# Layer 3's causal mask added to the scores on TensorE, and constant rows written in another block

## The reference

```python
q, k, v = x @ Wq.T + bq, x @ Wk.T + bk, x @ Wv.T + bv        # 16 heads of 8
scores = einsum('bhqd,bhkd->bhqk', q, k) / sqrt(8)
bias = -slopes[:, None, None] * abs(pos[:, None] - pos[None, :])
scores = scores + where(pos[:, None] >= pos[None, :], bias, -inf)
out = einsum('bhqk,bhkd->bhqd', softmax(scores), v)
return out.reshape(b, l, 128) @ Wo.T + bo
```

## Time and profile before

| | us |
|---|---|
| median of three runs | 2795.85 (2792.22 to 2800.66) |
| the profiled execution | 2813.61 |
| its span | 2811.9 |
| PE busy | 2098.0 (75%) |
| DVE busy | 1478.0 (53%) |
| ACT busy | 1163.6 (41%) |
| POOL busy | 395.0 (14%) |

### The profile page before, as it was taken

How to read it: one execution, slowest core, us unless ns; L and a number is a source line. 1 busy time by engine, 2 the same in 40 slices (tenths; PEclk the granted TensorE clock), 3 DMA queues, 4 the chain that set the end, 5 groups by cost and what they waited for, 6 DMA issues and landing times. The chain is left out here.

```text
span 2811.9 us, 41151 instructions
## 1 busy us (share of the span) xinstructions
PE 2098.0 (75%) x14039; PEld 1347.6 (48%) x14039; DVE 1478.0 (53%) x3920; ACT 1163.6 (41%) x2345; POOL 395.0 (14%) x474
## 2 busy tenths in 40 slices
PE   3313897546913889999999999996773068989976
PEld 2202796434912445555555555553662034444445
DVE  4628222252244656767777676773443455666524
ACT  0112453123410556666666666663221013555542
POOL 1260003513040341000000000000003520000000
PEclk9855898757955999999999999998997555897878
DMA  4310562114512100000000000001452131322001
GB/s 125 122 48 0 194 232 76 36 53 158 196 32 106 37 31 9 1 1 1 1 1 1 1 1 1 1 1 53 165 187 76 36 105 57 99 67 86 27 10 30
DMA packets 133972, 173.15 MB, mean 62 GB/s; under 512 B 16728, under 2 KB 93632, under 8 KB 133328
## 3 DMA queue, kind: packets, MB, share of 16 engines
q1 hardware_dynamic: 123104, 144.52, 15.9%
q0 software_dynamic: 10240, 20.99, 2.5%
q10 hardware_dynamic: 432, 5.11, 0.4%
HBM read 68.06 MB, written 45.15 MB: 40 GB/s over the span
## 5 line engine op out<-in xcount | busy, mean ns | idle before, releaser
L1845 ACT ACTIVATE t_p<-t_p,t_low 128x512 f32<-128x512 f32 x512 | 369.5, 722 | 327.1 <-DVE t_low L1916 321.1
L1916 DVE CUSTOM_DVE_ANT_0 t_p<-bank,L2t_skewed 128x512 f32<-128x512 f32 x512 | 332.6, 687 | 289.1 <-PE bank L1738 266.2
L127 PE MATMUL pair<-ident,t_p 128*128 128x128 f32 x2048 | 282.2, 280 | 18.7 <-ACT t_p L1845 6.6
L127 PEld LDWEIGHTS pair<-ident,t_p 128*128 128x128 f32 x2048 | 219.5, 141 | 115.6 <-issue 106.1
L2245 ACT ACTIVATE alibi_p<-pair 128x1024 f32<-128x1024 f32 (+1 forms) x192 | 168.8, 883 | 185.2 <-PE pair L2132 184.9
L2304 DVE CUSTOM_DVE_ANT_0 alibi_junk<-bank,alibi_later 128x512 bf16<-128x512 f32 (+1 forms) x256 | 150.8, 622 | 105.5 <-PE bank L2144 103.0
L1996 POOL COPY t_wide<-t_inverse 128x512 f32<-128x512 f32 x64 | 39.2, 613 | 893.5 <-DVE t_inverse L1932 884.6
L2144 PE MATMUL bank<-alibi_k_aug,alibi_q_aug 32*128 32x512 f32 (+1 forms) x256 | 107.7, 584 | 35.3 <-DMA alibi_k_aug<-aug_k 15.8
L1738 PE MATMUL bank<-t_k_hi,t_q_hi 64*128 64x512 f32 x512 | 129.7, 503 | 3.7 <-DVE t_low L1916 3.4
L1738 PEld LDWEIGHTS bank<-t_k_hi,t_q_hi 64*128 64x128 f32 x512 | 48.3, 185 | 162.2 <-issue 150.5
L1760 PE MATMUL pair<-t_pT,t_v 128*64 128x512 f32 x512 | 123.8, 605 | 1.5 <-DVE t_hT L1939 1.5
(11 more groups left out here) (478 smaller groups left out, 4458.4 us busy)
## 6 DMA issues: line engine op xcount, KB each, us to landing
L0moe_w<-L_packed SPq DMA_DIRECT2D x39, 578.0 KB, 3.2
L2moe_w<-L_packed SPq DMA_DIRECT2D x39, 450.0 KB, 2.9
L1moe_w<-L_packed SPq DMA_DIRECT2D x23, 578.0 KB, 3.3
alibi_q_aug<-aug_q SPq DMA_DIRECT2D x8, 1024.0 KB, 7.4
alibi_k_aug<-aug_k SPq DMA_DIRECT2D x8, 1024.0 KB, 7.6
L2t_skewed<-bias_table SPq DMA_DIRECT2D x16, 448.0 KB, 8.7
slots<-g ACTq DMA_DIRECT2D x3, 1664.0 KB, 10.2
L0moe_xs<-slots SPq DMA_DIRECT2D x39, 128.0 KB, 3.0
```

The source lines that it names most:

```text
L127: last = nc.tensor.transpose(out[0:piece.shape[1], j * P:j * P + piece.shape[0]], piece, ident[0:piece.shape[0], 0:piece.shape[0]])
L1845: nc.scalar.activation(p[:, u % RING, :], p[:, u % RING, :], ACT.Exp, bias=low[:, u % 16:u % 16 + 1], scale=-1.0, accum_out=sums[:, n % 2, ...
L1916: nc.vector.tensor_tensor_reduce(out=p[:, u % RING, :], in0=score_ps[h][:], in1=skewed[:, (n % PAIRS) * 2 + h, start:start + SEQ], scale=- ...
```

## The change

The constant rows are made and stored in `spread_bias_block` instead of `setup_block`, in tiles of their own: POOL's part behind the flip matrix, DVE's behind the spreading and before the turning, SP's four stores and the wait for them behind the wait for the skewed loads.

In layer 3 the maxima are plain reductions, one for a `tops_second`. The causal mask is added to every score job by PE: `hides` issues four parts of 128, 96, 64 and 32 columns (for each block of the job) in the job's own row strip, interleaved with the parts of the veils, and the last part adds one to `scored`. The full-array `hide` matmul, the tiles `later` and `junk`, and DVE's fills for them are gone. POOL makes `one`, `veil` and the new `shade` before its first `low_part`.

```diff
@@ setup_block @@
-        steady = [k.s[0:HEADS].rearrange("p t d -> p (t d)").rearrange("p (r n) -> p r n", r=8),
-                  k.xnT[0:HEADS].rearrange("p (r n) -> p r n", r=8)]
...
-            sp.wait_ge(rows_filled, 9)
-            for side in range(2):
-                for e in range(2):
-                    sp.dma_start(k.aug_dram[side][e, :, 24:32, :], steady[side]).then_inc(steady_stored, 16)
-            sp.wait_ge(steady_stored, 64)
...
-            for h in range(HEADS):
-                nc.gpsimd.memset(slope[:, 0, h:h + 1], high[h]).then_inc(slopes_set, 1)
-                nc.gpsimd.memset(slope[:, 1, h:h + 1], rest[h]).then_inc(slopes_set, 1)
-            pool.wait_ge(slopes_set, 2 * HEADS)
-            nc.gpsimd.affine_select(out=slope[:], in_=slope[:], compare_op=ALU.is_equal, fill=0.0, base=0,
-                                    pattern=[[0, 2], [-1, HEADS]], channel_multiplier=1).then_inc(slope_made, 1)
...
-            dve.wait_ge(slope_made, 1)
-            nc.vector.tensor_reduce(column[:, 0:2], slope[:], AX.X, ALU.add).then_inc(slope_summed, 1)
...
@@ spread_bias_block @@
+        steady = [st.sb(f"steady{j}", [HEADS, 8, SEQ])[:] for j in range(2)]
...
             sp.wait_ge(read, 16 * HEADS)
+            sp.wait_ge(rows_filled, 9)
+            for side in range(2):
+                for e in range(2):
+                    sp.dma_start(k.aug_dram[side][e, :, 24:32, :], steady[side]).then_inc(steady_stored, 16)
+            sp.wait_ge(steady_stored, 64)
...
+            dve.wait_ge(slope_made, 1)
+            nc.vector.tensor_reduce(column[:, 0:2], slope[:], AX.X, ALU.add).then_inc(slope_summed, 1)
+            dve.wait_ge(slope_summed, 1)
+            nc.vector.tensor_scalar(column[:, 2:4], column[:, 0:2], -1.0, None, ALU.mult).then_inc(slope_summed, 1)
+            dve.wait_ge(slope_summed, 2)
+            for j in range(2):
+                for row, col in ((1 - j, 2 * j), (3 - j, 2 * j + 1)):
+                    nc.vector.tensor_copy(steady[j][:, row, :], column[:, col:col + 1].to_broadcast([HEADS, SEQ])).then_inc(rows_filled, 1)
...
@@ alibi_attention_block, PE @@
+                w = 32 * (part + 1)
+                for c, a, e in regions(quad):
+                    for r in (2 * half, 2 * half + 1):
+                        ins = nc.tensor.matmul(flip_ps[u % 2][:, r % 2, a:a + w], one[rows(r), part, :], veil[rows(r), part, 0:w],
+                                               start=False, stop=True, skip_group_check=True)
+                if part == 3:
+                    ins.then_inc(flipped, 1)
...
                 bank = score_bank(s)
                 w = (t + 1) * P
                 nc.tensor.matmul(bank[:, 0:w], q_aug[rows(r), b % AUG, G, t * P:w], k_aug[rows(r), b % AUG, G, 0:w],
-                                 start=True, stop=True).then_inc(scored, 1)
+                                 start=True, stop=True, skip_group_check=True)
...
             def scores_first(b, s, r):
                 bank = score_bank(s)
-                if b == 0:
-                    pe.wait_ge(hide_laid, 1)
-                nc.tensor.matmul(bank[:].rearrange("p (g n) -> p g n", n=P), hide[:],
-                                 k.before[:].unsqueeze(1).to_broadcast([P, GROUPS, P]), start=True, stop=True)
                 for g in range(GROUPS):
-                    ins = nc.tensor.matmul(bank[:, g * P:(g + 1) * P], q_aug[rows(r), b % AUG, g, 0:P],
-                                           k_aug[rows(r), b % AUG, g, 0:P], start=False, stop=True,
-                                           skip_group_check=True)
-                ins.then_inc(scored, 1)
+                    nc.tensor.matmul(bank[:, g * P:(g + 1) * P], q_aug[rows(r), b % AUG, g, 0:P],
+                                     k_aug[rows(r), b % AUG, g, 0:P], start=(g == 0), stop=True, skip_group_check=True)
+
+            def hide(s, r, part, blocks, period, first):
+
+                out = score_ps[s % 2][:].rearrange("p (g n) -> p g n", n=period)[:, 0:blocks, first + 32 * part:first + P]
+                mask = shade[rows(r), part, 32 * part:P].unsqueeze(1).to_broadcast([32, blocks, P - 32 * part])
+                ins = nc.tensor.matmul(out, one[rows(r), part, :], mask, start=False, stop=True, skip_group_check=True)
+                if part == 3:
+                    ins.then_inc(scored, 1)
...
+            def hides(b, m, part):
+                s, G, kind, other = score_index(b, m), m // 6, m % 6, 2 * (1 - m % 2)
+                if b == 0 and m == 0 and part == 0:
+                    pe.wait_ge(veiled, 12)
+                if kind < 4:
+                    t = 3 - kind // 2
+                    hide(s, other, part, 1, SEQ, t * P)
+                    hide(s + 1, other + 1, part, 1, SEQ, t * P)
+                else:
+                    hide(s, other + G % 2, part, 2, 2 * P, P)
+                    if first_row(m) is not None:
+                        hide(s + 1, first_row(m), part, GROUPS, P, 0)
...
                     b, m = score_tick(n, j)
                     if 0 <= b < NB:
                         scores(b, m)
-                    if 0 <= n < NB:
-                        veils(n, j)
+                    for part in range(4):
+                        if 0 <= n < NB:
+                            veils(n, j, part)
+                        if 0 <= b < NB:
+                            hides(b, m, part)
@@ alibi_attention_block, VectorE @@
             def tops_one(b, s, G, r, t):
-                w, h = (t + 1) * P, 4 * G + r
+                h = 4 * G + r
                 dve.wait_ge(scored, s + 1)
-                nc.vector.tensor_tensor_reduce(out=junk[:, s % 2, 0:w], in0=score_ps[s % 2][:, 0:w], in1=later[:, SEQ - w:SEQ], scale=1.0,
-                                               scalar=-HUGE, op0=ALU.add, op1=ALU.max, accum_out=top[:, t, h:h + 1]).then_inc(maxed, 1)
+                nc.vector.tensor_reduce(top[:, t, h:h + 1], score_ps[s % 2][:, 0:(t + 1) * P], AX.X, ALU.max).then_inc(maxed, 1)
 
             def tops_second(b, s, G, r):
                 dve.wait_ge(scored, s + 1)
-                for g in range(2):
-                    h, half = 4 * (G + g) + r, slice(g * 2 * P, (g + 1) * 2 * P)
-                    ins = nc.vector.tensor_tensor_reduce(out=junk[:, s % 2, half], in0=score_ps[s % 2][:, half],
-                                                         in1=later[:, SEQ - 2 * P:SEQ], scale=1.0, scalar=-HUGE, op0=ALU.add,
-                                                         op1=ALU.max, accum_out=top[:, 1, h:h + 1])
-                ins.then_inc(maxed, 1)
+                nc.vector.tensor_reduce(top[:, 1, :].rearrange("p (g r) -> p g r", r=4)[:, G:G + 2, r],
+                                        score_ps[s % 2][:].rearrange("p (g n) -> p g n", n=2 * P), AX.X, ALU.max).then_inc(maxed, 1)
...
-            nc.vector.tensor_scalar(hide[:], k.ident[:], LOWEST, None, ALU.mult).then_inc(hide_laid, 1)
-            nc.vector.memset(later[:, 0:SEQ - P], 0.0).then_inc(later_laid, 1)
-            nc.vector.tensor_scalar(later[:, SEQ - P:SEQ], k.before[:], LOWEST, None, ALU.mult).then_inc(later_laid, 1)
-            dve.wait_ge(later_laid, 2)
@@ alibi_attention_block, GpSimd @@
+            nc.gpsimd.memset(one[:], 0.0).then_inc(cleared, 1)
+            nc.gpsimd.memset(veil[:], 0.0).then_inc(cleared, 1)
+            nc.gpsimd.memset(shade[:], 0.0).then_inc(cleared, 1)
+            pool.wait_ge(cleared, 3)
+            for r in range(4):
+                nc.gpsimd.affine_select(out=one[rows(r)], in_=one[rows(r)], compare_op=ALU.not_equal, fill=1.0, base=0,
+                                        pattern=[[-32, 4], [1, P]], channel_multiplier=-1).then_inc(veiled, 1)
+                nc.gpsimd.affine_select(out=veil[rows(r)], in_=veil[rows(r)], compare_op=ALU.is_ge, fill=LOWEST, base=0,
+                                        pattern=[[-32, 4], [1, P]], channel_multiplier=-1).then_inc(veiled, 1)
+                nc.gpsimd.affine_select(out=shade[rows(r)], in_=shade[rows(r)], compare_op=ALU.is_ge, fill=LOWEST, base=0,
+                                        pattern=[[32, 4], [-1, P]], channel_multiplier=1).then_inc(veiled, 1)
+            pool.wait_ge(veiled, 12)
             low_part(0, 0, q_cut, q_low)
             low_part(0, 1, k_cut, k_low)
             nc.gpsimd.memset(v_aug[:], 0.0).then_inc(ones_cleared, 1)
             pool.wait_ge(ones_cleared, 1)
             nc.gpsimd.memset(v_aug[:].rearrange("p e t h c -> p (e t h) c")[:, :, W:W + 1], 1.0).then_inc(ones_laid, 1)
-            nc.gpsimd.memset(one[:], 0.0).then_inc(cleared, 1)
...
```

More of the change, by code:

```diff
@@ L2071, in alibi_attention_block @@
         full, hi, lo = (st.sb(n, [P, 2, SEQ]) for n in ("full", "hi", "lo"))
-        later, junk = st.sb("later", [P, SEQ]), st.sb("junk", [P, 2, SEQ], BF16)
-        hide = st.sb("hide", [P, P], BF16)
-        one, veil = st.sb("one", [P, 4, P], BF16), st.sb("veil", [P, 4, P], BF16)
```

(46 more changed lines are left out.)

42 lines of the change are left out of this document (17 added, 25 removed).

## The result

The changed kernel took 2856.14 us (median of 4 runs, 2842.91 to 2862.26) beside 2795.86 of the kernel before: a ratio of 1.0207 (95% interval 1.0175 to 1.024), **+60 us** (+49 to +67) where +49 was forecast. Its profiled execution took 2851.98 us with a span of 2850.2, +38.4 against the span of before. So the two profiled executions stand nearer to each other than the medians: that of the kernel before took 18 us more than its median, that of the changed kernel 4 us less than its own.

A forecast was written before the change was run, and what follows sets the result against it. Setup was held by the constant-row stores, the attention's first 32 ticks by a PE-VectorE ping-pong, its 1.2 GHz middle by PE. Terms -17 + 7 + 22 + 21 + 7 + 9 = +49 on 2795.85 gave 2845 us; range 2813 to about 2905.

The forecast's parts named there:

- Constant rows out of setup, -17: Setup block: without the four stores it ends near 18.1 us instead of 35.0, -17 us, bounds -17 and -13.
- Into the bias block, 0: Bias block: making and storing the constant rows there costs 0, with 9 us of cover; +7 if stores took twice as long.
- Start of the attention, +7: Layer 3's attention start: GpSimd makes three masks before its first `low_part`, so the first scores come 7 us later.
- The loop of a tick: Layer 3's attention: a joint post makes each tick one closed loop; six ticks 13.9 us at 1.2 GHz, 11.0 at 2.4.
- First 32 ticks, +22: Attention ticks before the first exponentials, all at 1.2 GHz: 76 us against 54.4, +22 us.
- Ticks at 2.4 GHz, +0.20 each: Middle of layer 3's attention: 106 ticks at 2.4 GHz each 0.20 us longer, +21 us; bounds 0.08 and 0.4 each.
- Ticks at 1.2 GHz, +0.13 each: Middle of layer 3's attention: 54 ticks at 1.2 GHz each 0.13 us longer, +7 us; bounds 0 and +22.
- Clock, +9: Layer 3's attention: longer ticks leave PE less dense, 14 more ticks fall to 1.2 GHz, +9 us; bounds 0 and +60.
- 2 (masks cost nothing): Rival on layer 3's attention: slack takes the masks up, leaving -17 + 7, 2786 us; 5%.
- 1 (faster by the clock): Rival on layer 3's attention: masks fill idle strips, PE is granted 2.4 GHz throughout, 2780 us; 7%.
- 4 (the clock falls for most of the middle): Rival on the attention's middle: 160 ticks at 2.57 us, +82 in place of +37, 2890 us; 12%.
- 3 (strips don't overlap): Rival on PE's masks: added matmuls start one behind the other, about +35 us, 2880 us; 15%.

The follow-up runs named there:

- experiment 5: The changed kernel run again (2859.47 us, ratio 1.0237), and with GpSimd's first two low parts ahead of the masks' making (2847.82 us, ratio 1.021).
- Experiment 2: Kernel before with constant rows moved and both score jobs posted by the second's last matmul; old maxima, no masks on PE: 2833.49 us, ratio 1.0187.
- experiment 7: The changed kernel with all veils of a tick issued ahead of all its masks, not interleaved: 2843.87 us, ratio 1.0181.
- low parts early: The changed kernel with GpSimd's first two low parts ahead of the masks' making; on chip C 2826.92 us, ratio 1.0182.
- chip B: Chip on which the unaltered changed kernel was run again: 2859.47 us, ratio 1.0237 to the kernel before.
- The order alone: The kernel of Experiment 2, rows moved and one joint post without masks on PE: 2833.49 us, ratio 1.0187; again on another chip 2828.58 us, ratio 1.0187.
- experiment 3: The changed kernel with each tick's second score and its masks after the first score's masks and the veils, a post per bank: 2854.32 us, ratio 1.0224.
- experiment 6: Kernel before with constant rows moved and the veils between a tick's two scores, no masks on PE: 2771.98 us, ratio 0.9897.
- experiment 8: On one chip, The order alone again (2828.58 us, ratio 1.0187) beside the changed kernel with low parts early (2826.92 us, ratio 1.0182).
- The doubled kernel: The changed kernel with every added mask matmul issued twice, order unchanged: 2919.03 us, ratio 1.0488.
- the rows alone: Kernel before with only the constant rows moved as in the change, maxima and masks as before: 2771.47 us, ratio 0.996.

## Why the prediction was right

**Constant rows out of setup, -17:** -16.5, by both traces. The last fetch stayed hidden.

**Into the bias block, 0:** as long as before to within 0.1 us.

**Start of the attention, +7:** +7.3, and experiment 5 shows the mechanism.

**The loop of a tick:** six ticks forecast at 13.9 us at 1.2 GHz, 14.07 measured; the first tick 2.45 (forecast 2.46), 384 columns 2.07 (2.07). **First 32 ticks, +22:** +23.0. Experiment 2 splits it: 14.2 the order, 8.8 the masks' work.

**Ticks at 2.4 GHz, +0.20 each:** +0.25 in the profiled execution (1.77 to 2.01), and 2.00 to 2.02 in three others; with 110 ticks +27 where +21 stood. With whole ticks alone it is +0.18 to +0.22, so the size is right within the counting. The loop itself came to 2.07 against 2.05. The exponential, whose post comes later behind the masks (experiment 7), may add to it; that is argued and not isolated.

**Ticks at 1.2 GHz, +0.13 each:** +0.15, but the level was wrong: I took 2.44 us from one stretch of before, and all its stretches give 2.73. So 49 ticks ran at this clock, not 54: +7, as forecast.

**Clock, +9:** the pair of profiled executions denies it (0.79 before and 0.81 after in the middle). Without it the terms come to +48 and the spans to +38; of the 10 us between, 5 lie in the last 32 ticks (47.3 to 42.2, at a clock of 1.00, where I had said "as before"), 2 ahead of the attention and 2 in the middle. The runs affirm the term: with the masks a kernel had 39 us (chip C, low parts early) to 69 (chip B) more at 1.2 GHz than before. The terms above account for 23 + 7 of it, and on chip B for the 7 of the start too, which lie at a clock of 0.50. So 9 to 32 us are left, 3 to 11 ticks at 0.86, **+3 to +10**. The size was right, with luck in it, as the middle without any change there differed by 18 us between two traces. My reason was not right: I reasoned that longer ticks leave PE less dense. The order alone moves some 35 ticks to 1.2 GHz. The masks' work behind the joint post brings most of them back, all but some 3 on chip C and some 10 on chip B; yet with a post for each bank the same work moves some 45 ticks the other way (experiments 3 and 6). Nor is it long waits: PE's longest idle time in the middle was 1.24 us before, 0.68 in the change and 0.33 in experiment 3, and the clock fell in all three. And PE's busy share in the middle doesn't sort the kernels: 92% both before (302.6 of 327.9 us) and in experiment 8's order alone (333.6 of 361.1), 95% with masks, and 99% (388.45 of 392.2) in experiment 3, whose clock was the lowest. What the clock follows stays open.

**The sum:** -16.5 + 7.3 + 23.0 + 27 + 7 + 3 to 10 = +51 to +58, beside a measured +60 (+49 to +67). So the step that carried the forecast, one post for both banks making a tick one closed loop, is shown in the first 32 ticks and in the pace at 2.4 GHz. It is not shown that without it the masks would have been cheap.

**The rivals.** 2 (masks cost nothing) is refuted. Behind a joint post their work adds nothing to the whole (experiment 8, within 10 us), but with a post for each bank it adds 3.3% (experiment 3 beside 6). The two costs don't add up: either alone brings about nearly the whole loss. 1 (faster by the clock) fails, as the middle's clock was 0.81 to 0.85; 4 (the clock falls for most of the middle) fails for the change. It comes nearest in experiment 3, where 74 of 159 ticks ran at 1.2 GHz. 3 (strips don't overlap) fails: where both strips of a tick stream at once, the masks of six ticks are 4 x 320 + 1280 + 640 = 3200 columns one behind the other, 2.66 us at 0.83 ns and 14.2 over 32 ticks; one strip after the other they would be 5120, and 22.7. The doubled kernel took 14.2 more. The Trainium skill's floor of about 25 ns from start to start ("TensorE: Matmul & The Clock Gate", section "Wait — 56ns, not 53.3ns?") would put a tick's 7.3 added matmuls at 0.18 us at either clock; the doubling added 0.26 at 2.4 GHz and 0.44 in the first 32 ticks at 1.2. So the floor doesn't set the price here, the columns do. (The 0.48 us that I set against the floor for sixteen veils is their busy time; it is their starts, 0.27 us from first to last, 18 ns each, that lie below the floor.)

## What to carry to other kernels

When a last step is added behind two results that were posted one by one, and one post then serves both, price the lost overlap first: here the joint post alone cost as much as joint post and added work together (2828.6 us and 2826.9). But don't conclude that splitting the post again wins it back: with the work in place it won 13 us in the first 32 ticks and lost 32 in the middle. Test the parts in both orders, as the costs of two changes in one loop don't add up. Work the loop out by kind of tick and clock from the rows of before; in the first 32 ticks it came within 2% here. And take the clock from many runs, not from one profile: its share in one stretch of the same kernel can move the total by 18 us, a third of what the change does.

## What the runs showed of the hardware

- The granted clock in the middle of layer 3's attention differed by execution with no change there: 0.79 in the kernel before and 0.86 in the one with the rows alone (49 and 30 ticks at 1.2 GHz, 18 us in 328); the changed kernel had 0.81 and 0.83.
- The same 32 last ticks took 42 us at a clock of 1.00 in the changed kernel, 47 at 0.88 in the one before and 58 at 0.68 with the rows alone. In all kernels with masks on PE they ran at 0.96 or more, but also in one of the two executions of the order alone.
- The posts of PE's matmuls come in program order, though matmuls of other row strips start out of it: the veils of a tick start within 0.11 us, and the exponential that waits for the last of them starts 0.06 us after the end of a mask in another strip that was issued before it (0.69 us from the first veil at 2.4 GHz; 0.53 with no masks, and 0.41 with the second score behind the veils).
- A kernel in which PE was busy 99% of the middle, with no idle time above 0.33 us, had the lowest clock there, 0.70.
